# Three attentions rewritten: row maxima from the high halves in row groups of TensorE, both head pairs side by side

## The reference

```python
# xa0, D_K = 16
scores = jnp.einsum('bhqd,bhkd->bhqk', qh, kh) * scale
attn = jax.nn.softmax(scores, axis=-1)
out = jnp.einsum('bhqk,bhkd->bhqd', attn, vh)
...
# a1 (causal) and a2, D = 32
a = jax.nn.softmax(jnp.einsum('bhsd,bhtd->bhst', q, k) * D ** (-0.5), axis=-1)
if causal:
    mask = (jnp.arange(t)[None, :] > jnp.arange(s)[:, None]).astype(a.dtype)
    a = a * mask
o = jnp.einsum('bhst,bhtd->bhsd', a, v)
```

## Time and profile before

| | us |
|---|---|
| median of 3 runs | 4659.37 (4658.74 to 4666.88) |
| span of the profiled execution | 4666.5 |
| PE busy | 4034.3 (86%) |
| DVE busy | 2859.9 (61%) |
| ACT busy | 1944.0 (42%) |
| POOL busy | 912.1 (20%) |
| mean granted TensorE clock | 0.910 of 2.4 GHz |

### The profile page before, as it was taken

One profiled execution on the slowest core, in us unless ns is written; L12 is line 12 of the kernel. 1 busy time (PEld: TensorE's weight loads), 2 busy tenths in 40 slices (PEclk: granted clock), 3 DMA queues, 4 the chain that ended last, 5 costly groups with the idle time before them and its releaser, 6 DMA issues. The chain is left out here.

```text
span 4666.5 us, 65472 instructions
## 1 busy us (share of the span) xinstructions
PE 4034.3 (86%) x23278; PEld 1887.4 (40%) x23278; DVE 2859.9 (61%) x5627; ACT 1944.0 (42%) x3868; POOL 912.1 (20%) x369
## 2 busy tenths in 40 slices
PE   5999999628846999999996679999997669999999
PEld 2334333317732332333224423333333446666665
DVE  4787878371145787867754467777771555555554
ACT  0565656201101565656672325555563422222222
POOL 0000000002211000010104037777785300000000
PEclk7898989757966999999987879999998879999999
DMA  2000000016731000000000010000000110000000
GB/s 64 18 18 12 22 8 8 5 40 206 237 109 39 16 8 21 8 21 8 8 1 23 8 37 12 20 10 18 10 6 5 37 39 20 29 19 29 19 19 18
DMA packets 98523, 146.37 MB, mean 31 GB/s; under 512 B 28563, under 2 KB 84058, under 8 KB 91226
## 3 DMA queue, kind: packets, MB, share of 16 engines
q1 hardware_dynamic: 93658, 137.52, 9.4%
q0 software_dynamic: 4608, 5.57, 0.7%
HBM read 98.64 MB, written 9.18 MB: 23 GB/s over the span
## 5 line engine op out<-in xcount | busy, mean ns | idle before, releaser
L486 DVE TENSOR_REDUCE a_part_max<-a_wb 128x1 f32<-128x512 f32 (+1 forms) x2048 | 1167.9, 626 | 301.2 <-PE a_wb L558 291.9
L438 ACT ACTIVATE a_e<-a_sc 128x512 f32<-128x512 f32 (+1 forms) x1472 | 797.9, 598 | 805.9 <-PE a_sc L589 802.8
L558 PE MATMUL a_wb<-a_ks,a_qs 96*128 96x512 f16 (+1 forms) x2048 | 745.8, 371 | 49.6 <-DMA a_qs<-a_stage 28.0
L403 POOL TENSOR_TENSOR a_part_sum<-a_part_sum,a_e 128x2048 f32<-128x2048 f32 x128 | 581.3, 4541 | 141.2 <-ACT a_e L438 78.2
L438 ACT ACTIVATE xa_e<-xa_sc 128x512 f32<-128x512 f32 (+1 forms) x832 | 440.8, 599 | 366.1 <-PE xa_sc L589 365.6
L589 PE MATMUL a_sc<-a_qs,a_ks 97*128 97x512 f16 (+1 forms) x1472 | 546.3, 384 | 12.7 <-DMA a_qs<-a_neg_max 8.0
L486 DVE TENSOR_REDUCE xa_part_max<-xa_wb 128x1 f32<-128x401 f32 x1024 | 513.7, 567 | 61.8 <-PE xa_wb L558 56.5
L558 PEld LDWEIGHTS a_wb<-a_ks,a_qs 96*128 96x128 f16 x2048 | 199.9, 98 | 657.8 <-DVE a_part_max L486 474.0
L1437 ACT ACTIVATE moe_sg<-moe_gp 128x512 f32<-128x512 f32 (+1 forms) x216 | 128.6, 595 | 609.4 <-PE moe_up L1391 609.4
L1466 DVE TENSOR_TENSOR moe_hf<-moe_sg,moe_up 128x512 f32<-128x512 f32 (+1 forms) x216 | 148.2, 686 | 378.9 <-ACT moe_sg L1437 378.9
L558 PE MATMUL xa_wb<-xa_ks,xa_qs 96*128 96x401 f16 x1024 | 345.9, 350 | 17.1 <-DMA xa_qs<-xa_stage 11.7
(11 more groups left out here) (298 smaller groups left out, 4499.9 us busy)
## 6 DMA issues: line engine op xcount, KB each, us to landing
experts_w_up<-in_we SPq DMA_DIRECT2D x32, 1024.0 KB, 6.5
moe_w<-in_wm SPq DMA_DIRECT2D x18, 1088.0 KB, 5.0
experts_w_down<-in_we SPq DMA_DIRECT2D x32, 512.0 KB
a_qs<-a_stage SPq DMA_DIRECT2D x384, 32.0 KB, 1.9
a_ks<-a_stage SPq DMA_DIRECT2D x336, 32.0 KB, 1.9
xa_qs<-xa_stage SPq DMA_DIRECT2D x192, 32.0 KB, 1.9
experts_aw<-in_aw SPq DMA_DIRECT2D x16, 384.0 KB
xa_ks<-xa_stage SPq DMA_DIRECT2D x144, 32.0 KB, 1.9
```

The source lines that it names most:

```text
L403: pool.tensor_tensor(part_sum[:, :, :], part_sum[:, :, :], e[:, (nkt * n + kt) % ering, :, :], ALU.add).then_inc(part_added, 1)
L438: act.activation(e[:r, m % ering, j, :], sc[(HG * m + j) % NSC][:r, :], ACT.Exp, scale=scale).then_inc(exp_done, 1)
L486: dve.tensor_reduce(part_max[:, j, t, k:k + 1], src[:, :mxw], AX.X, ALU.max).then_inc(unit_taken, 1)
L558: last = pe.matmul(dst[:, :mxw], qs[:STACK, j, n % NQ, P * t:P * t + P], ks[:STACK, g % 2, j, mxs[k]:mxs[k] + mxw], start=True, stop=True)
```

## The change

The call and its results stay, and so do the numbers of scores, exponentials and value sums. These parts are new:

- Maxima are taken from the high halves alone. `qhi` and `khi` hold them by slot, so head j's matmul has 32 rows and stands on partitions 32j to 32j+31. A "pair" is two heads, two matmuls into a PSUM tile `mx` of two banks, and one DVE reduce over both. There are two such tiles. The two pairs of a query tile and key span are one entry of the work list, so four matmuls stand side by side in PE's order.
- The scores' stacks have 3*dk + 1 rows with the maximum's row first. In a1 and a2 that is 97 rows as before. In xa0 it is 49 rows, two heads in one column range, at partitions 0 and 64, and their two score matmuls stand side by side.
- Each value sum is cut into two halves of 256 columns (in diagonal tiles the part before the diagonal block and the block), with side work between. The weight sum of a tile follows the second half.
- K, Q and V projections and the turn use the ring `sc`, shared with the scores: three tiles in xa0, two in a1 and a2.
- ACT copies K and Q out of PSUM as f32 (`raw`, two slots), and also V, the turn and the spread. POOL makes the high and the low part. The maxima wait for the high part alone, not for the stacking DMAs.
- In a2 POOL adds 7 tiles an n in place of 8 and no longer clears its sum. The memset of the ones moves behind the K and Q units of the start.
- The weights of a head group are loaded two groups ahead in place of all at the start.

```diff
-        wb = [ps(f"wb{i}", [P, CH]) for i in range(NWB)]
+        mx = [ps(f"mx{i}", [P, 2, CH]) for i in range(2)]
...
+    NSC = 2 if own_sum else 3
...
+    per = 2 if dk == 16 else 1
+    parts = 3 * dk
+
+    def place(j):
+        return 64 * (j % per), j // per
+
+    def pairs(n, spans=range(nmx)):
+        return [("pair", n, t, h, c) for c in spans for t in range(TPC) for h in range(HG // 2)]
...
+        work = [[u] for u in work]
         if n + 1 < NC:
-            work += maxima(n + 1) + [("turn", n + 1)]
+            every = pairs(n + 1)
+            work += [every[i:i + HG // 2] for i in range(0, len(every), HG // 2)] + [[("turn", n + 1)]]
         if n + 2 < NC:
-            work.insert(16, ("q", n + 2))
+            work.insert(4, [("q", n + 2)])
         if 0 < n < NC - 1:
-            work[26:26], work[32:32] = [("divisors", n - 1)], [("divide", n - 1)]
+            work[7:7], work[9:9] = [[("divisors", n - 1)]], [[("divide", n - 1)]]
...
+        for half in range(2):
+            if n < NC:
+                order.append(("s", n, kt, 2 * half))
+                if per == 2:
+                    order.append(("s", n, kt, 2 * half + 1))
+            order += some_work(3 * half)
+            if n < NC and per == 1:
+                order.append(("s", n, kt, 2 * half + 1))
+            order += some_work(3 * half + 1)
+            if m and not passed((m - 1) // nkt, (m - 1) % nkt):
+                order.append(("pv", (m - 1) // nkt, (m - 1) % nkt, half))
+            order += some_work(3 * half + 2)
+        if m and own_sum and not passed((m - 1) // nkt, (m - 1) % nkt) and not on_pool((m - 1) % nkt):
+            order.append(("sum", (m - 1) // nkt, (m - 1) % nkt))
...
+                    pool.tensor_copy(high, raw[:, i % NR, :w]).then_inc(high_ready, 1)
+                    pool.wait_ge(high_ready, i + 1)
+                    pool.tensor_tensor(low[:, i % NST, :w], raw[:, i % NR, :w], high, ALU.subtract).then_inc(split_ready, 1)
...
+                if u[0] == "pair":
+                    n, t, h, c = u[1:]
+                    dve.tensor_reduce(part_max[:, 2 * h:2 * h + 2, t, c], src[:, :, :mxw], AX.X, ALU.max).then_inc(m_taken, 1)
...
+                elif u[0] == "divide":
+                    act.wait_ge(inverse_ready, u[1] + 1)
...
+                    act.activation(spread[:, :, :, :], inverse[:, :, :].unsqueeze(3).to_broadcast([P, TPC, HG, SLOT]),
+                                   ACT.Copy).then_inc(inverse_spread, 1)
...
+            def pair(u):
...
+                for i in range(2):
+                    rows = slice(SLOT * (2 * h + i), SLOT * (2 * h + i) + SLOT)
+                    last = pe.matmul(dst[:, i, :mxw], qhi[rows, n % NQ, P * t:P * t + P], khi[rows, g % 2, mxs[c]:mxs[c] + mxw],
+                                     start=True, stop=True)
+                last.then_inc(m_ready, 1)
...
+            for u in order:
+                if u in s_at and s_at[u] >= NSC:
+                    pe.wait_ge(s_taken, s_at[u] - NSC + 1)
+                if u in m_at and m_at[u] >= 2:
+                    pe.wait_ge(m_taken, m_at[u] - 1)
```

More of the change, by code:

```diff
@@ L255, in passed, with on_pool @@
         return causal and kt < TPC * (n % NCH)
[L258 to L273 removed]
+    def on_pool(kt):
+        return own_sum and not causal and 0 < kt < nkt - 2 and kt % 4 > 0
+    pool_kts = [kt for kt in range(nkt) if on_pool(kt)]
+    order = [("k", 0, 0), ("q", 0), ("k", 0, 1)]
+    for c in range(nmx):
+        order += pairs(0, [c]) + ([("k", 0, c + 2)] if c + 2 < len(kch) else [])
+        if c == 1:
+            order += [("v", 0, b) for b in range(nvb)] + [("q", 1)]
+    order.append(("turn", 0))
     during = []
@@ L283, in attention @@
         if n + 2 < NC:
-            work.insert(16, ("q", n + 2))
+            work.insert(4, [("q", n + 2)])
         if 0 < n < NC - 1:
-            work[26:26], work[32:32] = [("divisors", n - 1)], [("divide", n - 1)]
+            work[7:7], work[9:9] = [[("divisors", n - 1)]], [[("divide", n - 1)]]
         during.append(work)
-    after = [(u, n) for n in (NC - 2, NC - 1) for u in ("divisors", "divide")]
-    order = before + [u for work in during for u in work] + after
-    number = {u: i for i, u in enumerate(order)}
@@ new lines, in attention @@
+    order += [("divisors", NC - 2), ("divide", NC - 2), ("out", NC - 1), ("divisors", NC - 1), ("divide", NC - 1)]
+    s_at = {u: i for i, u in enumerate(u for u in order if u[0] in ("k", "q", "v", "s", "turn"))}
+    m_at = {u: i for i, u in enumerate(u for u in order if u[0] in ("pair", "divisors", "divide"))}
+    staged = {u: i for i, u in enumerate(u for u in order if u[0] in ("k", "q"))}
+    pv_at = {u[1:3]: i for i, u in enumerate(u for u in order if u[0] == "pv" and u[3] == 1)}
+    sum_at = {u[1:3]: i for i, u in enumerate(u for u in order if u[0] == "sum")}
```

556 lines of the change are left out of this document (290 added, 266 removed).

## The result

The changed kernel takes 4785.9 us in the median (4781.5 to 4797.0) beside 4662.9 for the kernel before on the same chip: a ratio of 1.027 (95% interval 1.0255 to 1.0287), 2.7% slower, where 4460 was forecast. The profiled execution spans 4779.7 us, 113.2 more than before. An n lasts 49.7 us in xa0, 67.7 in a1 and 52.0 in a2, where 42, 57 and 50 were forecast.

The account below looks back on a forecast made before the run. TensorE (PE), busy 86% of 4666.5 us, was taken as the bound. Savings of 74 (xa0), 72 (a1), 10 (a2) and 42 (start-ups) sum to 198, giving 4468 profiled and 4460 timed; range 4300 to 4640.

Parts of the forecast that it names:

- the 0.28 of a four in xa0: In xa0, four adjacent 32-row maxima overlap and with one change of shape take 0.28 us of PE.
- the change of shape of 0.09 to 0.10: On PE, each change of matmul tile shape costs 0.09 us, with row groups as with column groups.
- 42 for the start-ups: At the three attentions' starts, maxima no longer wait for the stacking DMAs, saving 42 us in all.
- Rival (1): On PE, row groups do not overlap, so the kernel gets slower, 4890 us; chance 0.10.
- the ring of two in a1: In a1, with two score tiles, the second score waits 0.2 to 0.3 us in places: 1 us a chunk.
- the saving of a1's maxima: In a1, maxima in fours of 32 rows take 6.1 us of PE a chunk instead of 14.1.
- The second pair's wait: PE waits for a four's second pair until earlier double reduces end: 3 us a chunk in xa0, 1 in a1 and a2.
- no bound: DVE's floor of double reduces, 29 us a chunk (a1: 36), does not limit the loops.
- The spread: PE's divide waits for the spread of the inverses, now queued behind exponentials on ACT: 1.0 us a chunk.
- rival (2): In xa0's loop, PE streams less and is granted 1.2 GHz for part of it: +130 to +190 us; chance 0.10.
- The sign set for this rival: A granted clock of xa0's loop below 0.85 would show that the clock had fallen.
- rival (3): More waits in all loops (double reduces, POOL's splits, ACT's copies): 2 us more a chunk, 4556 us; chance 0.15.

Follow-up runs that it names:

- f4: The changed kernel with the spread of the inverses back on DVE everywhere and pairs spread evenly in xa0 only: 4645.8 us, ratio 0.9956.
- h2: The changed kernel with the spread on DVE and three score tiles in a1 (a1's output not the attention's): 4673.3 us, ratio 1.003.
- h5: h2 with a1's maxima over 96 rows again, still in fours and double tiles: 4692.6 us, ratio 1.0071.
- g3: The kernel before with each of a1's maxima over 256 of its 512 columns, matmul and reduce both: 4595.3 us, ratio 0.9856.
- f1: The kernel before with a ring of two score tiles instead of three in a1 and a2: 4692.2 us, ratio 1.006.
- e1: The changed kernel with the spread of the inverses moved from ACT back to DVE everywhere: 4723.7 us, ratio 1.014.
- g2: The changed kernel with a1's maxima over all 96 stacked rows again, still in fours and with two score tiles: 4845.3 us, ratio 1.0385.

## Why the prediction was wrong

What held: the row groups overlap, the 0.28 of a four in xa0, the 0.32 of two scores, and the change of shape of 0.09 to 0.10 (0.10 in a1's timeline). The double reduce runs at a pace of 0.90, as worked out. Everything outside the loops of 15 gained 66, where the forecast has 52: 42 for the start-ups and 10 for the sixteenth chunks. Rival (1) did not happen.

Three steps failed: what PE loses to the double reduces, taken from mean distances in a chunk; the ring of two in a1, taken at 1 us a chunk; and the saving of a1's maxima, subtracted whole, as if the clock and PE's pace stayed what they were.

xa0: forecast -69 over 15 chunks, measured +50. Three terms make up 109 of the 119.
- The second pair's wait. I settled it at (2.35 - s)/2 with s = 1.67, the mean distance of side work in a chunk, some 12 times: 3 us a chunk. What failed is this s. Fours do not come at the mean distance. Where they stand one to a half tile, PE's own round is 1.17; the same formula gives 0.59 for it, and the row shows 0.63. VectorE's two reduces take 1.80 of each such round, so it sets the pace there, although "no bound" was right for the chunk as a whole. Of the 168 torn fours 99 have this gap of 0.6 to 0.7. Together they lose 101 us in 15 chunks instead of 45: +56. The 0.29 in the wait list seems to confirm the forecast's 0.34, and does not; it is the part of the gap in which the pipeline is empty.
- The spread: 25 instead of 15: +10.
- The clock, rival (2): 0.944 before, 0.89 after. That is 78 and 164 us at half speed; the 86 more cost half of themselves, an estimate of +43; no run isolates it. The sign set for this rival, a clock below 0.85 in xa0, did not show.

As a test of these sizes, f4: 695 - 129 (15 x 9.1 saved with the spread's 1.0 back, less 0.5 of ring wait) + 67 for pairs that cost as much as fours + 8 for its clock of 0.928 = 641; measured 644.

a1: forecast -68, measured +99; this is where most of the error lies, 167.
- The ring of two, priced at 1 us a chunk by the score's round trip at full clock, is 44 in 15 chunks (h2) instead of 15. The step forgot that projections and turns pass through the same two tiles, and that fours stand undivided between two scores.
- The spread is 22 instead of 15.
- The maxima: 8.0 us a chunk were subtracted, 120 in 15 chunks, and nothing of it came (h2 against h5). A four costs 0.43 instead of 0.38, which is 12 of the 120; the other 108 went to the clock and to ACT's pace. Rival (2) had the mechanism and the size (+130 to +190), but placed it in xa0, because the earlier trace rows show the half clock there, behind V's small f32 pieces. I had taken as a place of waits and did not ask what that stretch would look like with less for PE to do.
- Rows 8 speak against the forecast in a second way: passed tiles go at ACT's pace, so a saving of PE can't be kept there whole. In g3 about half of 105 us was kept. I subtracted all of it.

These are 29 + 7 + 120 = 156 of the 167. How the 108 divide between the clock and ACT's pace stays open. So does the share of the double reduces: 123 of a1's 240 fours are torn, with gaps of 73 us in all instead of the 15 forecast, but a part of these gaps lies where PE would have waited for ACT in any case, and no run isolates them.

a2: forecast -9, measured +30. The ring of two (14 in f1) and the spread (15 in e1) cost what I took for them, 15 each. The step that failed is again the second pair's wait, at 1 us a chunk: 152 of the 240 fours are torn, and their gaps add up to 70 us instead of 15. With the clock (0.995, now 0.982: some 10 by the same halving) that is more than the 39, so other terms must have cost less than forecast. No run parts them, and the split in a2 stays open.

So rival (3), more waits, and rival (2), the clock, came true together, (2) in a1 rather than in xa0. I had treated them as alternatives: each alone was priced to leave the kernel faster. They meet in the same tiles: going back to 96-row maxima and their better clock left the loop 40 us longer with a ring of two (g2) and 3 shorter with three tiles (h5 against h2). The range's upper end, 4640, came from adding neither to the other.

## What to carry to other kernels

Here a saving on TensorE was worth its full size only in the stretches where TensorE set the pace at full clock; so price it tile kind by tile kind, and for stretches paced by another engine ask first what clock they will be granted when less is left to do. Side work placed as one block between the users of a short ring is priced from start to start, not from the wait list, and with the distance at which such blocks really stand, not with the mean of a chunk. A ring must be counted with everything that passes through it (projections, turns), not with its main user alone. Where a rewrite has several parts, the split by stage tells which stage should keep which part: here xa0 took the row groups, spread evenly, and a1 its old form, and that version is 1.7% faster than before where the whole change is 2.7% slower.
